# Attention's last three units: each weighted sum in two halves of the queries, with two scores ahead of each half

## The reference, cut to what matters

```python
q = (x @ wq).reshape(bsz, toks, NH, HD)
k = (x @ wk).reshape(bsz, toks, NKV, HD)
v = (x @ wv).reshape(bsz, toks, NKV, HD)
scores = jnp.einsum('bqgrd,bkgd->bgrqk', qg, k) / jnp.sqrt(HD)
attn = jax.nn.softmax(scores, axis=-1)
out = jnp.einsum('bgrqk,bkgd->bqgrd', attn, v).reshape(bsz, toks, NH * HD) @ wo
x = _layernorm(x + out)
# then the feed-forward layer: of each block of 32 hidden units the one that a low-rank predictor picks
```

## Time and profile before

| | |
|---|---|
| median of three runs | 797.41 us (796.53 to 797.68) |
| the profiled execution's own time | 796.83 us |
| its span | 795.0 us |
| PE busy | 777.2 us, 98% of the span |
| DVE busy | 657.8 us, 83% |
| ACT busy | 390.3 us, 49% |
| loop of 29 units | from about 88 us to 380.55 us in the span |
| loop of the last three units | 380.55 us to 414.60 us |

### The profile page before, as it was taken

The page is one execution under the profiler, slowest core; times in us unless marked ns, Lnnn a source line. Parts: engine busy times, 40 slices in busy tenths (PEclk is TensorE's granted clock), DMA queues, the critical chain, the costliest instruction groups (busy, mean ns, idle before and its releaser), DMA issues.

```text
span 795.0 us, 13190 instructions
## 1 busy us (share of the span) xinstructions
PE 777.2 (98%) x4912; PEld 481.2 (61%) x4912; DVE 657.8 (83%) x842; ACT 390.3 (49%) x710; POOL 337.2 (42%) x445
## 2 busy tenths in 40 slices
PE   6999999999999999999999999999999999999995
PEld 5866533333333333333337788878878887888884
DVE  5578899999999999999226897988977897788764
ACT  4321588888888888888861331420310131102101
POOL 2213243754676456323411572444443344344432
PEclk9999999999999999999999999999999999999999
DMA  7693253344554454333407730440510031002001
GB/s 237 238 290 126 86 167 89 94 137 131 153 167 118 126 152 147 94 103 107 129 25 236 256 99 12 107 102 1 139 20 1 1 85 48 1 0 73 34 0 54
DMA packets 71816, 83.21 MB, mean 105 GB/s; under 512 B 34680, under 2 KB 38776, under 8 KB 71624
## 3 DMA queue, kind: packets, MB, share of 16 engines
q1 hardware_dynamic: 63920, 64.19, 27.3%
q0 software_dynamic: 7408, 16.81, 7.1%
q10 hardware_dynamic: 424, 1.38, 0.6%
HBM read 54.23 MB, written 28.05 MB: 103 GB/s over the span
## 4 chain that ended last, share of the span: by engine, by line
PE 93%; DVE 3%; DMA 2%; issue 1%; ACT 0%; SPq 0%; POOL 0%; POOLq 0%; DVEq 0%
PE ps_h L1378 20%; PE ps_pair L1396 19%; PE ps_st L692 12%; PE ps_st L677 10%; PE ps_pair L658 8%; PE ps_st L633 6%; PE ps_pv L692 6%; PE ps_pv L677 3%; PE ps_pv L633 2%; PE ps_pair L709 2%; PE ps_prep L1353 2%; PE ps_prep L1348 1%; DVE neg_max L551 1%; PE ps_pair L1363 1%; PE ps_prep L1340 1%; DMA yf<-x 1%
## 5 line engine op out<-in xcount | busy, mean ns | idle before, releaser
L551 DVE TENSOR_REDUCE neg_max<-ps_pair 128x2 f32<-128x1024 f32 x256 | 310.7, 1223 | 6.8 <-PE ps_pair L658 3.0
L517 ACT ACTIVATE probs<-ps_st 128x512 f32<-128x512 f32 x381 | 212.2, 599 | 28.6 <-PE ps_st L677 18.3
L1054 ACT ACTIVATE g_h<-picked 128x512 fp32r<-128x512 f32 x55 | 34.8, 632 | 217.1 <-DVE picked L1194 217.1
L677 PE MATMUL ps_st<-q,k 50*128 50x512 f32 x381 | 126.7, 494 | 0.2 <-ACT probs L517 0.2
L959 POOL TENSOR_TENSOR g_l<-picked,g_h 128x512 fp32r<-128x512 f32 x55 | 71.2, 1294 | 106.5 <-ACT g_h L1054 106.5
L658 PE MATMUL ps_pair<-k,q 48*128 48x512 f32 x512 | 107.8, 402 | 0.3 <-DVE neg_max L551 0.3
L692 PE MATMUL ps_st<-probs,v 128*32 128x256 f32 x1344 | 107.4, 391 | 0.0
L677 PEld LDWEIGHTS ps_st<-q,k 50*128 50x128 f32 x381 | 48.6, 183 | 75.7 <-ACT probs L517 56.2
L1378 PE MATMUL ps_h<-xt_h,w_l 128*128 128x512 f32 x224 | 89.0, 397 | 0.0
L1378 PE MATMUL ps_h<-xt_l,w_h 128*128 128x512 f32 x224 | 88.7, 396 | 0.0
L1378 PE MATMUL ps_h<-xt_h,w_h 128*128 128x512 f32 x224 | 88.7, 396 | 0.0
(11 more groups left out here) (177 smaller groups left out, 1344.9 us busy)
## 6 DMA issues: line engine op xcount, KB each, us to landing
operands<-parts POOLq DMA_DIRECT2D x20, 512.0 KB, 3.8
q<-operands SPq DMA_DIRECT2D x64, 128.0 KB, 2.6
sums<-stage SPq DMA_DIRECT2D x32, 256.0 KB, 2.8
x_raw<-xT SPq DMA_DIRECT2D x16, 256.0 KB, 5.0
k<-operands SPq DMA_DIRECT2D x64, 64.0 KB, 2.3
q<-operands SPq DMA_DIRECT2D x64, 64.0 KB, 2.5
att<-sums SPq DMA_DIRECT2D x16, 256.0 KB
yf<-x SPq DMA_DIRECT2D x4, 1024.0 KB, 7.1
```

The source lines that it names most:

```text
L517: nc.scalar.activation(probs[kt % 2][:, r], score_bank(i)[:], ACT.Exp, scale=float(HD) ** -0.5).then_inc(exp_done, 1)
L551: nc.vector.tensor_reduce(neg_max[:, at:at + 2], ps_max[pair % 2][:], AX.X, ALU.max, negate=True).then_inc(max_red, 1)
L677: nc.tensor.matmul(score_bank(i)[:], k_[n % QR][64 * a:64 * a + ROWS, kt * P:(kt + 1) * P], q[n % QR][64 * a:64 * a + ROWS, j, :], start=T ...
```

## The change

In the loop of the last three units the whole `weigh` becomes two halves of 256 queries. The first half stands behind the score tiles r = 0, 1, the second behind r = 2, 3; the projection's four matmuls stay behind both. `weigh` increments `pv_done` with the second half. The last `weigh`, of step 127, stays whole, and nothing outside this loop changes.

```diff
             for n in range(NU - AHEAD, NU):
                 for kt in range(TT):
                     step = n * TT + kt
-                    for r in range(REP):
-                        scores_t(n, kt, r)
-                    weigh(step - 1, slice(0, S))
+                    scores_t(n, kt, 0)
+                    scores_t(n, kt, 1)
+                    weigh(step - 1, slice(0, S // 2))
+                    scores_t(n, kt, 2)
+                    scores_t(n, kt, 3)
+                    weigh(step - 1, slice(S // 2, S))
                     project_out(step - TT * (NU - AHEAD))
             weigh(NT // REP - 1, slice(0, S))
```

## The result

The changed kernel takes 801.05 us (799.77 to 801.26) against 797.54 us (796.53 to 797.71) of the kernel before: a ratio of 1.0046 with a 95% interval of 1.0034 to 1.0058, so slower by 2.7 to 4.6 us. Each of the two is a median of four runs here, so the kernel before stands at 797.54 us and not at the 797.41 us of three. Forecast were 801.1 us. The profiled execution took 799.77 us, 2.9 us more than that of before; 800.5 us were forecast for it.

What follows compares the result with a forecast made beforehand. PE was taken as the bound. Eleven steady steps at + 0.34 us (+ 3.8 us) less 0.1 us at step 116 gave + 3.7 us, so 797.41 + 3.7 = 801.1 us, range 798.9 to 802.3.

Steps and rivals of the forecast that it cites:

- The bound: Last three units: PE is busy throughout, and the chain behind the last `weigh` moves one for one with the twelve steps.
- The halves: 11 steady steps: two halves of the sums take 1.14 us against 0.99 us whole, + 0.15 us a step.
- The lone pairs: 11 steady steps: two separate score pairs take 0.86 us against 0.67 us for the group, + 0.19 us a step.
- rival B: Score pairs standing alone cost only 0.33 us, so only the halves cost: + 1.5 us, 798.9 us; chance 0.08.
- The sum of a steady step: Steps 117 to 127: 0.15 + 0.19 = + 0.34 us each, + 3.7 to + 3.8 us over 11 steps.
- Step 116: First of the twelve steps: the first half partly fills PE's stall for the last row maximum, - 0.1 us.
- Its other case: Step 116: if the first half could start at 380.98 us, the step would gain 0.3 us.
- The sign for the last `weigh`: End of the stage: the last `weigh` starts at 418.2 to 418.4 us instead of 414.60, distances behind it kept.
- The moved waits: Steps with a unit's copy: copy some 0.1 us later, last Exp still in time with 0.36 us cover, cost nothing.
- C: Unit boundaries and step 116: the copy delays the last Exp past its cover, 1.5 us on top, 802.6 us; chance 0.05.
- D: PE's busy time hides 5.1 us of waits for ACT that halves fill: - 1.4 us, 796.0 us; chance 0.04.
- E: Halves and groups cost their columns alone, only step 116 counts: - 0.1 to - 0.3 us, 797.2 us; chance 0.03.

Runs made afterwards that it cites:

- lone pairs: Kernel before, with the whole `weigh` set between the two pairs of score tiles, projection behind the second; ratio 1.0029 to the kernel before.
- six groups: Changed kernel, with two of the projection's four matmuls behind each half of the sums; ratio 1.0083 to the kernel before.

## Why the prediction was right

*The bound.* PE alone sets the stage, and the chain behind moves one for one. Right: the distances behind the last `weigh` stayed.

*The halves, + 0.15 us a step.* Right in size (0.57 us a half), but my words for it, "the sums in halves", put it to the cut. The kernel with both halves together shows that it belongs to the second group of sums: + 0.015 us for the cut, the rest for standing apart.

*The lone pairs, + 0.19 us a step.* Right: 0.43 us each, and 0.198 us a step in the kernel that has only them. This was the term that decided between slower and no change. Whoever prices a pair by the spacing within a group of two (0.33 us) gets rival B, 798.9 us, and "no change". The measured interval leaves that out.

*The sum of a steady step.* 0.34 us forecast, 3.124 - 2.785 = 0.34 us measured; eleven times, 3.7 us (3.73; the prediction's sum took 3.8, which rounds 11 x 0.34 = 3.74 up).

*Step 116.* Mis-sized: - 0.1 us forecast, - 0.27 us measured. The step that failed is "ACT starts the Exps of step 116 at 381.09, so that one is done just before". That row says when the next Exp began, not when the last one had ended. The trace before has a row with the end:

```profile
379.86 1.09 ACT L517 ACTIVATE probs<-ps_st 128x512 f32<-128x512 f32 x2
```

Step 115's last Exp ended at 379.86 + 1.09 = 380.95, so a half could start when the pair ahead of it was done, 0.43 us after 380.55. ACT then stood idle for 0.14 us for want of a score tile. In the changed kernel the first half starts 0.44 us into the step (380.42 against 379.98), with nothing waited for. The prediction's sign for it, a start 0.55 us or more into the step (381.1 to 381.2, where the step began at 380.55), did not come true. Its other case, a start at 380.98 with - 0.3 us in all, is the one that came. For the stage it makes 3.73 - 0.27 = + 3.46 us, and + 3.44 was measured; my 3.7 was too high by 0.17 us at step 116 and by the rounding.

*The time.* That 801.1 us was met within 0.05 us is in part luck. The medians differ by 801.05 - 797.54 = 3.5 us, not 3.7, and the kernel before came out 0.13 us higher than the 797.41 us on which the forecast was built. The sign for the last `weigh`, a start at 418.2 to 418.4 us, was missed: it started at 417.46, since the stage began 0.57 us early and was 0.2 us shorter than forecast. Counted from the stage's first score pair it starts 37.48 us in instead of 34.05, + 3.43 us.

*The moved waits, costed at nothing.* Right in the changed kernel, where no first half waits. ACT idles for 1.03 to 1.05 us a step (1.06 forecast), and the last Exp of the step with the copy ends at 395.13 + 0.59 = 395.72, with the half at 396.06, in these rows of ACT and PE:

```profile
386.78 0.60 ACT L517 ACTIVATE probs<-ps_pair 128x512 f32<-128x512 f32 x1 [1.04 <-PE ps_st L677]
```

```profile
394.64 0.60 ACT L488 ACTIVATE stage<-ps_pv 128x512 f32<-128x512 f32 x1
395.13 0.59 ACT L517 ACTIVATE probs<-ps_st 128x512 f32<-128x512 f32 x1
```

```profile
396.06 0.64 PE L692 MATMUL ps_pv<-probs,v 128*32 128x256 f32 x8
```

That is 0.34 us of cover (0.36 forecast). The kernels with lone pairs and with six groups overran it.

*The rivals.* B fell with the pairs' 0.43 us. C isn't in the changed kernel. D's 796.0 us lies outside what was measured, and the weight loads of two `weigh`s in the kernel before speak against its 5.1 us as waits:

```profile
395.76 0.16 PEld L692 LDWEIGHTS ps_pv<-probs,v 128*32 128x32 f32 x8 [0.37 <-ACT probs L517]
398.55 0.16 PEld L692 LDWEIGHTS ps_pv<-probs,v 128*32 128x32 f32 x8 [0.37 <-issue]
```

The idle time ahead of the load is 0.37 us whether an Exp is named as its end or nothing is ("issue"), and from step 117 on it is 0.36 or 0.37 us ahead of every `weigh` of this loop, so the Exps named didn't hold these loads back. E fell as the price of the change, though its estimate for the cut holds. The prediction's "The trace disagrees, with 0.15 us a step" compared it with a half that stands apart, which pays for a second group and not for the cut.

## What to carry to other kernels

Where TensorE is the bound and works in several array shapes, count the groups between changes of shape before counting matmuls: here each costs 0.14 to 0.19 us, so interleaving more finely is a loss unless it fills a stall longer than what the added groups cost (0.34 us a step here; only step 116, at 2.28 us against the 1.66 us of its work, had one). Price a piece of work by a row where it stands in the same surroundings as it will have, from start to start; the spacing inside a longer group is the wrong row. And for when an engine is done, read the end of the row before, not the start of the one behind.

## What the runs showed of the hardware

In this stage the fixed cost comes with the change of shape, not with the number of matmuls, the cut or the waits. From pairs: 0.43 us alone, 0.67 for two. From sums: 0.57 for a lone half, 1.00 for two together, so 0.14 us. From projections: 0.66 for two, 1.13 for four, so 0.19 us. Parting along any of the three boundaries gave it. Going over to other operands and another bank within a shape doesn't: in the loop of 29 units two score tiles are followed by two of the other kind (L677, then L658), both on two row groups, and the two pairs take 0.33 and 0.32 us, no more than two pairs of one kind. The Trainium skill's page "TensorEngine Tiling (Array Packing)", section "Key Properties", has the cause as a drain at a change of tiling mode; the runs agree that the change costs, and the size is theirs.

The weight loads show where in time part of it lies. These are the first three loads of a group of projections in the kernel before, and after them the matmul that the second load belongs to:

```profile
388.41 0.19 PEld L709 LDWEIGHTS ps_pair<-wo_h,xt_l 128*128 128x128 f32 x1 [0.84 <-issue]
388.52 0.19 PEld L709 LDWEIGHTS ps_pair<-wo_h,xt_h 128*128 128x128 f32 x1
388.75 0.19 PEld L709 LDWEIGHTS ps_pair<-wo_l,xt_h 128*128 128x128 f32 x1
```

```profile
388.75 0.39 PE L709 MATMUL ps_pair<-wo_h,xt_h 128*128 128x512 f32 x1
```

Inside the group a load starts 0.23 us ahead of its matmul (388.52 for 388.75). The group's first load starts only with its matmul, at 388.41, though the loads had been idle for 0.84 us and the profile shows nothing that was waited for. So it is in every group of this stage in all nine traces: first load and first matmul start within 0.02 us of one another. The first matmul then takes 0.34 us to the second, the ones inside the group 0.23. That it is the drain that holds the load back, and not that the late load is itself the cost, no run here separates.

Also, PE's busy share is no sign of useful work: in the stretches quoted it was 100% at 2.785 as at 3.12 us a step.
